# The head of a two-layer attention program: x loaded first, six buffers, queries turned from PSUM, late constants

## The reference, cut to what matters

```python
qkv = x.reshape(b, hw, c) @ qkv_w + qkv_b                 # x is group-normalised before
attn = einsum('bqd,bkd->bqk', q * SCALE, k)
rel_h = einsum('bhwc,hkc->bhwk', r_q, Rh)                  # r_q: q as (32, 32, 64)
rel_w = einsum('bhwc,wkc->bhwk', r_q, Rw)
x = x + softmax(attn + rel_h + rel_w) @ v @ proj_w + proj_b
```

## Time and profile before

| What | us |
|---|---|
| runs: median of 3 (lowest, highest) | 2991.14 (2991.06, 2993.95) |
| the profiled execution's own time | 2980.41 |
| its span | 2978.4 |
| TensorE busy | 2666.8 (90%) |
| VectorE / ScalarE / GpSimd busy | 2062.7 / 2051.0 / 1726.2 |
| mean granted TensorE clock | 0.968 |

### The profile page before, as it was taken

One profiled execution on the slowest core, in us unless ns is written; L12 is line 12 of the kernel. 1 busy time (PEld: TensorE's weight loads), 2 busy tenths in 40 slices (PEclk: granted clock), 3 DMA queues, 4 the chain that ended last, 5 costly groups with the idle time before them and its releaser, 6 DMA issues.

```text
span 2978.4 us, 69056 instructions
## 1 busy us (share of the span) xinstructions
PE 2666.8 (90%) x29020; PEld 1562.5 (52%) x29020; DVE 2062.7 (69%) x3769; ACT 2051.0 (69%) x2427; POOL 1726.2 (58%) x1181
## 2 busy tenths in 40 slices
PE   6899988999889998899988999889988999889995
PEld 3455644556446564465635656356553555536562
DVE  6775767767676667767777587675776758767574
ACT  6676856868568586685766866577666687668683
POOL 5364764747547375573755746457464665647463
PEclk8899999999999999999999999899999999999997
DMA  3000001000100001000010000100002000010000
GB/s 120 23 2 2 2 12 54 2 1 2 34 32 2 1 2 43 23 2 1 2 43 23 2 1 2 44 23 2 1 2 65 2 2 1 1 44 2 2 2 22
DMA packets 32756, 48.15 MB, mean 16 GB/s; under 512 B 5152, under 2 KB 32032, under 8 KB 32448
## 3 DMA queue, kind: packets, MB, share of 16 engines
q1 hardware_dynamic: 30944, 43.13, 4.4%
q10 hardware_dynamic: 1504, 0.61, 0.1%
HBM read 30.95 MB, written 12.58 MB: 15 GB/s over the span
## 4 chain that ended last, share of the span: by engine, by line
PE 45%; POOL 17%; DVE 16%; issue 11%; ACT 10%; DMA 0%; POOLq 0%; ACTq 0%; SPq 0%; DVEq 0%
POOL pl L994 16%; PE ps L547 10%; PE ps L881 7%; PE ps L671 5%; PE ps L842 4%; PE ps L851 4%; PE ps L806 4%; PE ps L844 3%; DVE mxp L950 3%; ACT qa L655 2%; DVE stats L1110 2%; DVE x L1106 2%; ACT p L926 2%; PE ps L1085 2%; ACT ph L912 2%
## 5 line engine op out<-in xcount | busy, mean ns | idle before, releaser
L994 POOL TENSOR_TENSOR pl<-p,ph 128x1024 f16<-128x1024 f32 (+2 forms) x672 | 1088.3, 1632 | 426.1 <-ACT ph L912 418.2
L950 DVE TENSOR_REDUCE mxp<-ps 128x1 f32<-128x512 f32 (+2 forms) x1344 | 778.5, 625 | 258.4 <-PE ps L806 253.0
L926 ACT ACTIVATE p<-ps 128x1024 f32<-128x1024 f32 (+1 forms) x672 | 640.5, 953 | 170.4 <-PE ps L851 169.1
L912 ACT ACTIVATE ph<-p 128x1024 f16<-128x1024 f32 (+1 forms) x672 | 669.3, 996 | 21.4
L881 PEld LDWEIGHTS ps<-v,ph 128*128 128x128 f16 x9600 | 506.2, 97 | 130.9 <-issue 29.9
L881 PE MATMUL ps<-v,ph 128*128 128x65 f16 (+1 forms) x9600 | 531.0, 194 | 18.7 <-POOL pl L994 18.7
L881 PE MATMUL ps<-v,pl 128*128 128x65 f16 x4800 | 509.0, 192 | 0.0
L881 PEld LDWEIGHTS ps<-v,pl 128*128 128x128 f16 x4800 | 446.7, 99 | 0.0
L994 DVE TENSOR_TENSOR pl<-p,ph 128x512 f16<-128x512 f32 (+1 forms) x336 | 284.2, 846 | 183.8 <-ACT ph L912 182.5
L851 PE MATMUL ps<-qc,kc 65*128 65x512 f16 (+3 forms) x1344 | 381.8, 365 | 0.0
L686 POOL TENSOR_TENSOR v<-o,v 128x384 f16<-128x384 f32 x128 | 113.3, 890 | 442.1 <-ACT o L682 442.1
(11 more groups left out here) (188 smaller groups left out, 5152.9 us busy)
## 6 DMA issues: line engine op xcount, KB each, us to landing
xin<-in_x SPq DMA_DIRECT2D x8, 1536.0 KB, 7.0
x<-in_x SPq DMA_DIRECT2D x8, 1536.0 KB, 7.1
out<-x SPq DMA_DIRECT2D x16, 768.0 KB, 3.6
qc<-rowt SPq DMA_DIRECT2D x96, 2.0 KB
o<-in_L_conv_qkv_w SPq DMA_DIRECT2D x2, 576.0 KB, 9.3
p<-in_L_conv_qkv_w SPq DMA_DIRECT2D x1, 576.0 KB, 10.8
x<-in_L_attn_Wq SPq DMA_DIRECT2D x1, 576.0 KB, 11.8
x<-in_L_attn_Wk SPq DMA_DIRECT2D x1, 576.0 KB, 12.5
```

Of the source, the lines that this page charges most:

```text
L912: self.nc.scalar.activation(m.ph[:, i % RING, :, 0:w], m.p32[:, i % RING, :, 0:w], ACT.Copy).then_inc(self.s["hi"], 1)
L926: nc.scalar.activation(m.p32[:, i % RING, :, 0:w], m.ps[:, 2 * (i % 2):2 * (i % 2) + 2, 0:w], ACT.Exp, scale=SCALE).then_inc(s["exp"], 1)
L950: nc.vector.reduce_max(m.mxp[:, h % 2, kh, qt:qt + 1], m.ps[:, bank, 0:w], AX.X).then_inc(s["free"], 1)
L994: engine.tensor_tensor(m.pl[:, i % RING, part, 0:w], m.p32[:, i % RING, part, 0:w], m.ph[:, i % RING, part, 0:w], ALU.subtract).then_inc(s ...
```

## The change

Only the first image's head is touched; `held` of later images gives the two temporaries of before, and they keep their order of products.

1. SP loads x first, then `c_proj_1`, `c_fc_1`; the four rel loads come after weight piece 2. Staging places 0 to 2 are now in `p32`, and `cpin` in `m.o`.
2. TensorE transposes x before the FFN factors; those of `c_proj_1` go to bank 7 before the means, those of `c_fc_1` to banks 1 to 3 after the variances and the rel matmuls. Their copies on ScalarE and VectorE move with them.
3. Image 0's normalised units have six temporaries (`held(n)` = `hT`/`lT`, block n // 2), so `normalise_dve` no longer waits; VectorE's low parts come after units 3 and 5.
4. Queries' high halves are turned by ScalarE straight from PSUM with the bias added, head by head; VectorE's `pair_low` of a query head waits for its turn. Pair 3 of image 0 has banks 0 and 1, and `before` is (0, 0, 0, 0, 4, 6).
5. The high halves of pieces 5 to 7 and the low halves of pieces 4 to 7 come behind all pairs; the value bias is made ahead of the pairs. TensorE waits for the bias only, and for the rest in `ready`, at token tile 5.
6. Image 0's four groups of relative-position products go with tiles 2 to 5 and not 0 to 3.

```diff
 # Prologue.sync
-        sp.dma_start(self.c1in, d.c_fc_1.rearrange("(i p) a -> p i a", p=P)).then_inc(s["ffn_in"], 16)
-        sp.dma_start(self.cpin, d.c_proj_1).then_inc(s["ffn_in"], 16)
         sp.dma_start(self.m.xin[:, :, :], d.x_tiles[0]).then_inc(s["first_in"], 16)
-        for i, r in enumerate((d.rel_h, d.rel_h, d.rel_w, d.rel_w)):
-            sp.dma_start(self.rel2[:, i, :], r).then_inc(s["rel_in"], 16)
+        sp.dma_start(self.cpin, d.c_proj_1).then_inc(s["ffn_in"], 16)
+        sp.dma_start(self.c1in, d.c_fc_1.rearrange("(i p) a -> p i a", p=P)).then_inc(s["ffn_in"], 16)
...
             sp.dma_start(self.stage[i % self.NS], src).then_inc(self.loads[i % self.NS], 16)
+            if i == NC_ - 1:
+                for j, r in enumerate((d.rel_h, d.rel_h, d.rel_w, d.rel_w)):
+                    sp.dma_start(self.rel2[:, j, :], r).then_inc(s["rel_in"], 16)
 # Prologue.scalar
-        act.wait_ge(s["cp_mm"], NF)
-        nc.scalar.activation(m.cp[:, :, :], m.ps[:, 4, 0:NF * FA]...).then_inc(s["cp_out"], 1)
-        act.wait_ge(s["c1_mm"], NF)
-        for r in range(2):
-            nc.scalar.activation(m.c1[r * FA:(r + 1) * FA, :], m.ps[0:FA, 1:4, :]..., ACT.Copy).then_inc(s["c1_hi"], 1)
         for n in range(2 * NC_):
             act.wait_ge(norm.s["transposed"], norm.s.at("transposed", n + 1))
             norm.copy(act, n, n)
+        act.wait_ge(s["cp_mm"], NF)
+        nc.scalar.activation(m.cp[:, :, :], m.ps[:, 7, 0:NF * FA]...).then_inc(s["cp_out"], 1)
         for i in range(self.NS):
             self.weight_high(act, i)
         for n in range(2 * NC_):
             norm.high(act, n)
+        act.wait_ge(s["c1_mm"], NF)
+        for r in range(2):
+            nc.scalar.activation(m.c1[r * FA:(r + 1) * FA, :], m.ps[0:FA, 1:4, :]..., ACT.Copy).then_inc(s["c1_hi"], 1)
         act.wait_ge(s["biases_in"], 16 * 6)
         for i in range(2 * NPAIR):
-            if self.NS + i < len(self.pieces):
-                self.weight_high(act, self.NS + i)
-            qkv.pair_high(act, i)
-            if i < NPAIR:
-                for parity in range(2):
-                    act.wait_ge(qkv.s["hi"], qkv.s.at("hi", 2 * i + parity + 1))
-                    dst, src = qkv.turned(0, i, parity)
-                    nc.scalar.activation(dst, src, ACT.Copy).then_inc(qkv.s["turned_hi"], 1)
-        act.wait_ge(s["lo_done"], len(self.pieces))
+            for parity in range(2):
+                qkv.pair_high(act, i, (parity,))
+                if i < NPAIR:
+                    dst, _ = qkv.turned(0, i, parity)
+                    rows = own(parity)
+                    nc.scalar.activation(dst, qkv.out2(i)[rows, :].rearrange("p (h w) -> p w h", w=IMG), ACT.Identity,
+                                         bias=m.bqk[rows, i:i + 1]).then_inc(qkv.s["turned_hi"], 1)
+        for i in range(self.NS, len(self.pieces)):
+            self.weight_high(act, i)
 # Prologue.vector
         for n in range(2 * NC_):
             norm.normalise_dve(dve, n)
-            if n % 2 == 1:
-                norm.low_dve(dve, n)
+            if n == 3:
+                norm.low_dve(dve, 1)
+        norm.low_dve(dve, 3)
+        norm.low_dve(dve, 5)
...
         for i in range(2 * NPAIR):
-            if 4 + i < len(self.pieces):
-                self.weight_low(dve, 4 + i)
-            qkv.pair_low(dve, i)
+            for parity in range(2):
+                if i < NPAIR:
+                    dve.wait_ge(qkv.s["turned_hi"], 2 * i + parity + 1)
+                qkv.pair_low(dve, i, (parity,))
...
-        nc.vector.reduce_sum(m.f2sum[:, :], m.cf2[:, :], AX.X)
+        nc.vector.reduce_sum(m.f2sum[:, :], m.cf2[:, :], AX.X).then_inc(s["const_dve"], 1)
+        for i in range(4, len(self.pieces)):
+            self.weight_low(dve, i)
 # Prologue.tensor
         pe.wait_ge(s["lo_done"], NC_)
         for i in range(2 * NPAIR):
             if i == 1:
                 pe.wait_ge(s["rel_out"], 1)
+            if i == 2:
+                pe.wait_ge(s["c1_lo"], 1)
+            if i >= 4:
+                pe.wait_ge(qkv.s["turned_hi"], 2 * (i - 2))
             qkv.pair_products(pe, i, channel_ready=norm.ready if i == 0 else None)
-        pe.wait_ge(s["lo_done"], len(self.pieces))
+        pe.wait_ge(s["bias_lo"], 1)
         pe.wait_ge(s["made"], 1)
-        pe.wait_ge(s["const_dve"], 1)
+
+    def ready(self, pe):
+        pe.wait_ge(self.s["lo_done"], len(self.pieces))
+        pe.wait_ge(self.s["const_dve"], 1)
 # FirstNorm
+    def held(self, n):
+        return (self.m.hT, self.m.lT)[n % 2][:, n // 2, :].bitcast(F32)
...
-        if n >= 2:
-            self.low_wait(dve, n - 2)
 # build
+            if b == 0:
+                w.qkv0.bank, w.qkv0.before = (6, 4, 2, 0, 4, 2), (0, 0, 0, 0, 4, 6)
+            w.with_v = ((0,), (1,), (2,), (3,), (), (), (), ()) if b else ((), (), (0,), (1,), (2,), (3,), (), ())
...
+                if t == 5 and not before:
+                    prologue.ready(pe)
```

More of the change, by code:

```diff
@@ L127, in __init__ @@
         self.nc, self.m, self.d, self.norm, self.qkv, self.stored = nc, m, d, norm, qkv, stored
-        self.stage = [m.o[:, 0:3, :], m.o[:, 3:6, :],
-                      m.p32[:, 0:2, :, :].rearrange("p a b c -> p (a b c)")[:, 0:3 * C].rearrange("p (a b) -> p a b", a=3),
-                      m.x[:, 0:3, :], m.x[:, 3:6, :]]
+        held = m.p32[:, :, :, :].rearrange("p a b c -> p (a b c)")[:, 0:9 * C].rearrange("p (n a b) -> p n a b", n=3, a=3)
+        self.stage = [held[:, 0], held[:, 1], held[:, 2], m.x[:, 0:3, :], m.x[:, 3:6, :]]
         self.pieces = []
@@ L324, in tensor @@
         pe.wait_ge(s["ident_made"], 1)
+        pe.wait_ge(s["first_in"], 16)
+        for n in range(2 * NC_):
+            norm.transposes(pe, n, n).then_inc(norm.s["transposed"], 1)
         pe.wait_ge(s["ffn_in"], 32)
         for i in range(NF):
[L327 to L334, removed]
-                pe.wait_ge(s["c1_hi"], 2)
-            if n == 4:
-                pe.wait_ge(s["cp_out"], 1)
-            norm.transposes(pe, n, n).then_inc(norm.s["transposed"], 1)
+            nc.tensor.transpose(m.ps[:, 7, i * FA:(i + 1) * FA], self.cpin[:, i * P:(i + 1) * P], m.ident[0:FA, 0:FA]).then_inc(s["cp_mm"], 1)
         pe.wait_ge(s["group_made"], NC_)
         norm.means(pe, 6).then_inc(norm.s["mean_mm"], 1)
+        pe.wait_ge(s["cp_out"], 1)
         norm.variances(pe, 7).then_inc(norm.s["var_mm"], 1)
@@ L346, in tensor @@
                              start=True, stop=True).then_inc(s["rel_mm"], 1)
+        for i in range(NF):
+            nc.tensor.transpose(m.ps[0:FA, 1 + i // 4, (i % 4) * P:(i % 4 + 1) * P], self.c1in[:, i, :], m.ident[:, :]).then_inc(s["c1_mm"], 1)
         pe.wait_ge(s["lo_done"], NC_)
@@ L389, in __init__ @@
         self.mean_g, self.dev, self.tvar, self.veps, self.rstd, self.shift = (m.small[:, i, 0:NC_] for i in range(6))
-        self.temp = [buf[:, NC_ - 1, :].bitcast(F32) for buf in (m.hT, m.lT)]
+    def held(self, n):
+        return (self.m.hT, self.m.lT)[n % 2][:, NC_ - 1, :].bitcast(F32)
     def unit(self, n):
@@ L459, in normalise @@
             act.wait_ge(s["lo"], s.at("lo", n - 1))
-        self.nc.scalar.activation(tiles(self.temp[n % 2]), self.unit(n), ACT.Identity, scale=self.rstd[:, c:c + 1],
+        self.nc.scalar.activation(tiles(self.held(n)), self.unit(n), ACT.Identity, scale=self.rstd[:, c:c + 1],
                                   bias=self.shift[:, c:c + 1]).then_inc(s["normed"], 1)
@@ L465, in high @@
         act.wait_ge(self.s["normed"], self.s.at("normed", n + 1))
-        self.nc.scalar.activation(self.m.xin_hi(c, 4 * hf, 4 * hf + 4), tiles(self.temp[n % 2]), ACT.Copy).then_inc(self.s["hi"], 1)
+        self.nc.scalar.activation(self.m.xin_hi(c, 4 * hf, 4 * hf + 4), tiles(self.held(n)), ACT.Copy).then_inc(self.s["hi"], 1)
     def low(self, pool, n):
@@ L471, in low @@
         pool.wait_ge(self.s["hi"], self.s.at("hi", n + 1))
-        self.nc.gpsimd.tensor_tensor(self.m.xin_lo(c, 4 * hf, 4 * hf + 4), tiles(self.temp[n % 2]), self.m.xin_hi(c, 4 * hf, 4 * hf + 4),
+        self.nc.gpsimd.tensor_tensor(self.m.xin_lo(c, 4 * hf, 4 * hf + 4), tiles(self.held(n)), self.m.xin_hi(c, 4 * hf, 4 * hf + 4),
                                      ALU.subtract).then_inc(self.s["lo"], 1)
@@ L485, in normalise_dve @@
         c = n // 2
-        if n >= 2:
-            self.low_wait(dve, n - 2)
-        self.nc.vector.tensor_scalar(tiles(self.temp[n % 2]), self.unit(n), self.rstd[:, c:c + 1], self.shift[:, c:c + 1],
+        self.nc.vector.tensor_scalar(tiles(self.held(n)), self.unit(n), self.rstd[:, c:c + 1], self.shift[:, c:c + 1],
                                      ALU.mult, ALU.add).then_inc(self.s["normed"], 1)
@@ L500, in subtract @@
         eng.wait_ge(self.s["hi"], self.s.at("hi", n + 1))
-        engine.tensor_tensor(self.m.xin_lo(c, 4 * hf, 4 * hf + 4), tiles(self.temp[n % 2]), self.m.xin_hi(c, 4 * hf, 4 * hf + 4),
```

(3 more changed lines are left out.)

25 lines of the change are left out of this document (12 added, 13 removed).

## The result

| | before | changed |
|---|---|---|
| median us (runs) | 2985.18 (11) | 2969.45 (11) |
| lowest to highest | 2973.71 to 2993.95 | 2963.46 to 2979.09 |
| the profiled execution: time, span | 2980.41, 2978.4 | 2972.85, 2970.8 |

The ratio is 0.9953, 95% interval 0.9937 to 0.9969: 14.0 us faster, between 9.3 and 18.8. The forecast was 14.9 off the median shown then (2991.14, three runs); more runs of before brought that median to 2985.18.

The account below looks back on a forecast made before the run. TensorE is busy nine tenths of the span, so only how early the first image's work begins counts. Gains 4.0 - 0.1 + 0.7 + 9.3 + 1.0 = 14.9 off median 2991.14 give 2976.2 us, range 2970 to 2984.

Parts of the forecast that it names:

- x first: Start of the head: x's load, put first in its queue, lands at 10.6 us instead of 14.6, gaining 4.0.
- Statistics: From x's landing to the first normalisation: c_proj transposes fill a TensorE gap; normalisation at 27.5 against 31.40, 0.1 lost.
- Six buffers: Image 0's normalised units: normalisations no longer wait in twos for low parts; 0.7 us gained.
- Clock at pair 0: TensorE's first pair: clock rises near 35 us, last six products run at the high clock, pair 0 ends at 37.2.
- Turns and pairs: ScalarE's pair loop: turns from PSUM cost 1.12 us, not 1.94; with the new pair order, 9.3 gained.
- rival (a): ScalarE's query turns cost 1.94 us from PSUM too; 4.9 lost, gain 10.0, time 2981.1; chance 0.11.
- Tail: From the last pair to the first rel copy: 11.2 us instead of 12.2, gaining 1.0.
- VectorE's cover: Before the first rel low part: VectorE's four moved low halves end at 67.2, leaving 1.6 us of cover.
- Rival (c): After the head: the gain is given back before the end, less than 6 us stays, about 2988; chance 0.07.

Follow-up runs that it names:

- the repetition: The changed kernel as it stands, run once more beside runs of before; median 2968.84 us (12 runs), ratio to before 0.9955.
- halves in the loop: The changed kernel with weight high halves 5 to 7 and low halves 4 to 7 back before the pairs' copies; pair 0 to maximum 44.5 us against 46.5.
- old banks: The changed kernel with image 0's pairs in the banks and low-part waits of before; pair 0 to last pair 24.3 us, 5.0 more; span 2966.1.
- small loads behind: The changed kernel with six small bias and factor loads issued by SyncE behind the fifth weight piece; x landed 7.4 us after issue, rel copy 62.82.
- unit 0 on VectorE: The changed kernel with unit 0's low part on VectorE, not POOL, units 0 and 1 finished first; first product 2.7 us after first normalisation, against 4.5.
- halves behind V1: The changed kernel with ScalarE's last three high halves behind its copies of V0 and V1; pair 0 to maximum 45.3 us against 46.5 and 45.9.
- edits together: The changed kernel with small loads behind, unit 0 on VectorE and the weight halves spread; median 2969.21 us (6 runs), ratio to before 0.9950.

## Why the prediction was right, point by point

- **x first.** Forecast 10.6, bounds 7.9 and 13.2; measured 11.8 and 11.4. The term was over-sized by 1: I gave ScalarE's loads 0.5 us of x's time, they take 3 to 4 (7.4 to landing without them, 10.4 to 11.6 beside them). With the rule that an engine goes round robin between its queues (the Trainium skill, DMA: Bandwidth & Descriptors, Queues, rings and completion order) these two numbers agree: x was not alone.
- **Statistics.** 16.8 from landing to normalisation before, 16.9 forecast, 16.3 and 15.6 measured. c_proj does fill the gap. Gained at the normalisation 3.3 and 4.4 in two executions, forecast 3.9.
- **Six buffers.** This step failed. I had the first product at 30.5, 3.0 behind the first normalisation, and the end of the last low part 6.3 behind it; they came 4.5 and 7.4 behind. POOL's two low parts, side by side with VectorE's normalisation of unit 3 and its low part, made these 1.38 and 1.64 instead of 0.54 and 0.69. The row was there to be read: in before, VectorE's 1.22 beside POOL's low part, which I called a wait for POOL and then let vanish.
- **Clock at pair 0.** Forecast a rise near 35; it came near 38.3 in one execution and near 29.6 in the other. (The fall in before was misread too: 0.63 in the slice from 25 to 26 puts it at 25.3, not 25.6.) The last six products at the high clock were a guess between, and pair 0 came 2.3 late or 1.1 early. The first product's lateness of 2.0 and 1.0 against 30.5 is in both.
- **Turns and pairs.** Forecast 1.12 per turn, 19.6 from pair 0 to the last pair; measured 1.10 and 19.36, before 28.88 (70.70 less 41.82). This is 9.5 of the gain, and rival (a), with its price of 4.9, is what the run with turns from SBUF shows: 5.0 (6 x 0.83 is 5.0 too, not 4.9). The sentence of the Trainium skill on non-contiguous access of PSUM (SBUF — State Buffer, Door 1) is on matmuls; carried over to ScalarE's reads it does not hold here: 1097 ns turned, 1108 in order.
- **Tail.** Forecast 11.2 with a clock between the levels; measured 11.15 where the clock fell to 0.50 as V2's products began, and 9.57 in the repetition where it stayed high. ScalarE is done with the halves 5.54 behind the last pair, at 64.42 (forecast 5.8). The bias made ahead of the pairs and the later place of the relative-position groups are in no run of their own. That the halves' new place costs 2 us against the old one was not among my steps, since I compared only whole tails.
- **VectorE's cover.** Forecast 1.6; in the changed kernel VectorE waited 1.66 before the first rel low part. In the repetition the cover was used up to the last: its halves ended at 65.78, the first rel copy at 65.83. That the maximum came 17.0 behind the rel copy there, instead of 15.95, is not VectorE's doing but TensorE's, which stopped for 2.68 us and then ran at the low clock, so that ScalarE's copies waited twice (0.54 and 0.37; the last section has the stop).
- **Rival (c).** The profile seemed to speak for it (12.8 at the mark, 7.5 at the end). Repetition and ratios speak against it.

The sum of 14.9 was met by 14.0 (9.3 to 18.8) and 13.4 (9.5 to 17.3), the second from the ratio 0.9955. That it came so near is in part luck. The terms of x and of the normalised units promised some 1 and 1.5 us too much, and the clock, at which I guessed, is some 4 of the 5 us by which the mark differs between two executions of the same kernel: the gain there was 12.85 in one and 17.85 in the other. The large term, turns and pairs, was right in mechanism and size.

## What to carry to other kernels

Cost a moved piece against the place it comes from, not only against the sum: the weight halves were hidden in part where they stood and bare where they went. When buffers take waits away, look at what will then run side by side; a row that is slow beside another engine is the price of that. And where one kernel's executions differ by more than the change, split the span into stretches with the same instructions before reading a single pair of profiles.

## What was unexpected of the hardware

VectorE's normalisation of 512 columns (float32, one tensor read from SBUF) took 0.54 us alone and 1.38 beside POOL's subtraction, and its own subtraction 0.69 and 1.64. For the pair of shared ports that the Trainium skill describes (SBUF — State Buffer, Who interferes with whom) the trace agrees, in that one waits for the other for most of an instruction.

TensorE's granted clock rose near 29.6 in the repetition of the changed kernel, before the first product of pair 0 at 31.46. The same happened in four of the nine variants (halves in the loop, old banks, small loads behind, unit 0 on VectorE); in the six other executions the rise came 2.6 to 5.9 us behind the first product, with the same work ahead of it in all but small parts. Windows of TensorE in that execution (length, busy us, granted clock, DMA, GB/s), and its timeline:

```profile
28.00:29.00 1.00, 1.00 (x6) 0.50 0.06 23
29.00:30.00 1.00, 0.26 (x2) 0.70 0.00 0
```

```profile
25.48 1.11 PE L341 MATMUL ps<-ph 63*128 63x63 f32 x4
26.52 2.74 PE L344 MATMUL ps<-ident,pl 128*32 128x128 f32 x12
31.46 1.02 PE L554 MATMUL ps<-xin,wqkv_hi 128*128 128x512 f16 x4 [2.20 <-DVE xin L508]
```

All that TensorE did just ahead of the rise are small fp32 products and the twelve transposes of c_fc. The sentence of the Trainium skill that transposes don't count as busy (TensorE: Matmul & The Clock Gate, Part 4) does not fit these transposes, unless the small products alone were enough; this was not separated, and these transposes are float32, where the page's measured one is bf16. In the profiled changed kernel the same work ended at 30.3 without a rise.

The twelve transposes took 2.69 us where the record grants the full clock in before, and 2.74 at a granted 0.50 here: they show no difference between the levels; and in before, four of x's transposes take 1.12 us at 14.62 and 0.65 at 141.66, both at a granted 1.00. Whether the record of the first microseconds is right stays open.

TensorE stops in the middle of a list without a wait that the profile shows. Chain of waits, changed kernel again, in the third group of relative-position products (44 of its 96 done):

```profile
69.83 0.65 PE ps L645 x44
70.47 2.68 issue
73.16 0.73 PE ps L645 x52
```

The changed kernel (2.08 us, up to 77.55) and six of the variants stop at the same product, for 1.9 to 3.5 us; before, halves in the loop, halves behind V1 and edits together do not. In the two executions of the changed kernel the load of x for the residual (1536 KB) moves at up to 407 GB/s just before the stop, and a 16 KB load on the queue that the page calls "instruction" starts at 70.88 (75.22 in the changed kernel). In all eight executions TensorE goes on 2.3 to 2.6 us after such a load's start. It would fit that TensorE had to wait for its next instructions, whose load was late beside that of x; this is a guess, and no run here tried it. In the changed kernel the stop cost the first maximum nothing, in the repetition 1.1 us.
